# Softmax-free attention with an FP4 gate: one store and eight loads for the reciprocals of a group, in place of four and sixteen

## The reference

```
xn = layernorm(src)
# attention branch, 16 heads of 64
Q = elu(xn @ Wq + bq) + 1 ;  K = elu(xn @ Wk + bk) + 1 ;  V = xn @ Wv + bv
KV = einsum('bshd,bshm->bhdm', K, V)
Z  = 1 / (einsum('bshd,bhd->bsh', Q, K.sum(axis=1)) + 1e-6)
o  = einsum('bshd,bhdm,bsh->bshm', Q, KV, Z)
x  = layer_norm(xn + o @ Wo + bo)
s  = layer_norm(x + gelu(x @ W1 + b1) @ W2 + b2)
# gate branch: rows and weights rounded to FP4 in blocks of 16
g  = silu( fp4_linear( silu(fp4_linear(xn, w_gate)) * fp4_linear(xn, w_up), w_down ) )
out = src + s * g
```

## Time and profile before

| | us |
|---|---|
| median of 3 runs | 1647.81 (1647.04 to 1648.1) |
| the profiled execution | 1644.95 |
| its span, first to last instruction | 1643.2 |
| TensorE busy | 1604.9 (98%) |
| VectorE busy | 1280.4 (78%) |
| ScalarE busy | 980.1 (60%) |
| GpSimd busy | 783.3 (48%) |

### The profile page before, as it was taken

The page is one execution under the profiler, slowest core; times in us unless marked ns, Lnnn a source line. Parts: engine busy times, 40 slices in busy tenths (PEclk is TensorE's granted clock), DMA queues, the critical chain, the costliest instruction groups (busy, mean ns, idle before and its releaser), DMA issues.

```text
span 1643.2 us, 30638 instructions
## 1 busy us (share of the span) xinstructions
PE 1604.9 (98%) x10977; PEld 1440.9 (88%) x10977; DVE 1280.4 (78%) x2485; ACT 980.1 (60%) x1770; POOL 783.3 (48%) x750
## 2 busy tenths in 40 slices
PE   7999999999899999999999999999999999999997
PEld 6878888888789998999999999989899989999897
DVE  6785664554788797888888887879788888878797
ACT  6665666655564747565665647474656656574743
POOL 4564543434242635444444536364455444363636
PEclk9999999999999999999999999999999999999999
DMA  7422323331501111133121112111121321111110
GB/s 227 136 84 86 104 78 106 103 109 57 186 15 53 52 53 52 53 111 91 47 68 53 52 53 107 53 52 53 52 60 61 104 87 58 53 52 53 52 53 26
DMA packets 92515, 123.46 MB, mean 75 GB/s; under 512 B 13503, under 2 KB 60747, under 8 KB 91342
## 3 DMA queue, kind: packets, MB, share of 16 engines
q1 hardware_dynamic: 92366, 121.51, 23.1%
HBM read 86.86 MB, written 34.62 MB: 74 GB/s over the span
## 4 chain that ended last, share of the span: by engine, by line
PE 68%; DVE 13%; DMA 7%; issue 5%; SPq 3%; ACT 3%; POOL 2%; DVEq 0%; POOLq 0%; ACTq 0%
PE QH L81 11%; PE QH L82 11%; PE QH L83 10%; PE AC L81 5%; PE AC L82 4%; PE AC L83 4%; DMA zb<-z_scratch 4%; PE GU L81 4%; PE GU L83 4%; PE GU L82 4%; DVE QH L1828 2%; PE TT L831 2%; DVE rl L1837 2%; SPq L408 2%; DMA z_scratch<-dn_s 1%
## 5 line engine op out<-in xcount | busy, mean ns | idle before, releaser
L2309 POOL TENSOR_TENSOR hb<-hb,rs_h 128x704 f32<-128x704 f32 x64 | 89.0, 1391 | 206.3 <-DVE rs_h L1680 206.3
L1248 ACT ACTIVATE hb<-GU 128x352 f32<-128x352 f32 x128 | 59.2, 463 | 214.3 <-PE GU L83 214.3
L1201 ACT ACTIVATE rh<-QH 128x512 fp32r<-128x512 f32 x256 | 151.2, 598 | 58.2 <-DVE QH L1828 53.2
L81 PE MATMUL GU<-wgh,xqh 128*128 128x352 f32 x512 | 169.8, 332 | 3.1 <-DVE hb L1673 3.1
L2315 POOL TENSOR_TENSOR hb<-hb,sn_h 128x64 f32<-128x64 f32 x64 | 18.8, 293 | 319.5 <-DVE hb L1685 319.5
L83 PE MATMUL GU<-wgh,xql 128*128 128x352 f32 x512 | 165.0, 322 | 0.0
L82 PE MATMUL GU<-wgl,xqh 128*128 128x352 f32 x512 | 164.9, 322 | 0.0
L1843 DVE TENSOR_TENSOR rl<-QH,rh 128x512 fp32r<-128x512 f32 x128 | 86.0, 682 | 85.8 <-ACT rh L1201 83.7
L81 PE MATMUL AC<-Mh,rh 128*128 128x256 f32 x512 | 145.9, 285 | 1.4 <-ACT rh L1201 0.6
L81 PE MATMUL AC<-w2h,rh 128*128 128x256 f32 x512 | 145.7, 285 | 0.0
L82 PE MATMUL AC<-Ml,rh 128*128 128x256 f32 x512 | 142.4, 278 | 0.0
(11 more groups left out here) (234 smaller groups left out, 5586.0 us busy)
## 6 DMA issues: line engine op xcount, KB each, us to landing
zb<-z_scratch SPq DMA_DIRECT2D x256, 128.0 KB, 3.0
xa<-in_L_attn_src SPq DMA_DIRECT2D x16, 512.0 KB, 4.2
xt_scratch<-xth SPq DMA_DIRECT2D x32, 256.0 KB, 2.7
xt_scratch<-xtl SPq DMA_DIRECT2D x32, 256.0 KB, 3.0
xb<-in_L_attn_src SPq DMA_DIRECT2D x16, 512.0 KB, 4.2
xnTh<-xt_scratch SPq DMA_DIRECT2D x32, 256.0 KB, 4.8
xnTl<-xt_scratch SPq DMA_DIRECT2D x32, 256.0 KB, 5.6
out<-x SPq DMA_DIRECT2D x15, 512.0 KB, 6.6
```

Source lines behind the costliest of these rows:

```text
L81: e.matmul(outp, lh, rh, start=start, stop=False, skip_group_check=check)
L1201: e.activation(RH[j % 4][:], src, ACT.Copy).then_inc(S[sem], 1)
L1248: e.activation(HB[i % 3][:, hf * HALF:(hf + 1) * HALF], gu_bank(i, hf)[:, 0:HALF], ACT.Tanh, scale=0.5).then_inc(S["th"], 1)
L2309: e.tensor_tensor(hb, hb, spread(rs_h[i % 2][:], 44), ALU.mult).then_inc(S["hin"], 1)
```

## The change

The four stores of a group become one over all 128 partitions of `dn_s`, with the partitions that hold no head; `z_scratch` has 32 rows for a group instead of 16, and row 16 to 31 are never read. The two loads of a block become one, whose source is two rows, each repeated 64 times. The waits count 16 for a DMA accordingly. Nothing is moved on the other engines.

```diff
-    z_dram = nc.dram_tensor("z_scratch", [NG, 16, 512], F32, kind="Internal").ap()
+    z_dram = nc.dram_tensor("z_scratch", [NG, 32, 512], F32, kind="Internal").ap()
             def z_out(g):
                 w.wait_ge(S["zi"], 2 * g + 2)
-                for t in range(4):
-                    e.dma_start(z_dram[g, :, t * 128:(t + 1) * 128], dn_s[32 * t:32 * t + 16, :]).then_inc(S["zo"], 16)
+                e.dma_start(z_dram[g].rearrange("h (t c) -> t h c", t=4), dn_s[:]).then_inc(S["zo"], 16)
             def z_in(g, j):
-                w.wait_ge(S["zo"], 64 * (g + 1))
+                w.wait_ge(S["zo"], 16 * (g + 1))
                 w.wait_ge(S["zq"], 8 * g + j - 3)
-                for s in range(2):
-                    e.dma_start(ZB[j % 4][64 * s:64 * s + 64, :],
-                                z_dram[g, 2 * j + s].unsqueeze(0).broadcast_to([64, 512])).then_inc(S[f"zb{j % 4}"], 16)
+                e.dma_start(ZB[j % 4][:], z_dram[g, 2 * j:2 * j + 2].unsqueeze(1).broadcast_to([2, 64, 512])).then_inc(S[f"zb{j % 4}"], 16)
             def den_inverse(g):
                 w.wait_ge(S["dn"], g + 1)
-                w.wait_ge(S["zo"], 64 * g)
+                w.wait_ge(S["zo"], 16 * g)
             def z_mul(g, j):
-                w.wait_ge(S[f"zb{j % 4}"], 32 * (2 * g + j // 4 + 1))
+                w.wait_ge(S[f"zb{j % 4}"], 16 * (2 * g + j // 4 + 1))
```

## The result

The changed kernel took 2168.72 us, median of four executions (2165.18 to 2169.65), beside 1647.95 us for the kernel before (1647.04 to 1648.32): a ratio of 1.3157, 95% interval 1.3134 to 1.318. The profiled execution took 2169.65 us, 1.75 us of it beside the span.

A forecast was written before the change was run, and what follows sets the result against it. TensorE, 98% busy, was taken as the bound, its chain passing through each group's reciprocals. Span 1643.2 + 515 (loads on two engines) + 24 (clock) = 2182 us, 2187 us as run time; range 2110 to 2330.

The forecast's parts named there:

- The bound: In every group the chain leaves TensorE through the reciprocals; a stall of TensorE pushes the kernel's end back by nearly as much.
- Two engines and four: New load (2 against 128) runs on two engines, new store (4 against 128) on four; with small clock price, chance 0.78.
- the rival in which only the store is cut and a load keeps 16 engines: Store over four engines, loads over 16: some 0.3 us won a group, 1643 us; chance 0.04.
- 85 ns a row: One engine's time for a 2 KB row of the zb loads, ends 82 and 107; last product 32.2 us later, 515 us.
- The store, gain 0: One store into z_scratch lands when the fourth did before: gain 0, ends 0.4 us gained or lost.
- What lies beside: TensorE has no work to do ahead during the slow loads, so 32.2 us a group go on the path.
- The clock: TensorE's clock probably falls to 1.2 GHz between products; its return costs 1.5 us a group (0 to 3.9), 24 us.
- the rival of sixteen engines: Loads run on sixteen engines after all, 0.7 us a block; 9 us gained, 1639 us (1634 to 1643); chance 0.10.
- The rival in which the clock stays low through most of the 56 us: Low clock behind each group's last product costs 10 us and more a group: 2320 us; chance 0.06.

The follow-up runs named there:

- every kernel of the table: Thirteen kernels, the change and twelve follow-ups, each set beside the kernel before by shift of the last product and of the rest; measured differences from -19.1 to 590.3 us.
- with four engines: Changed kernel's loads, each head's row stored twice by four stores so the load's source leads with 4: 1835.46 us, ratio 1.1137 to the kernel before.
- The experiments with 4, 8 and 16: Changed kernel's eight loads, row copies stored by four stores so the source leads with 4, 8 or 16: 1835.46, 1689.28 and 1666.80 us.
- the kernel with 60 zero matmuls: Changed kernel with zero matmuls filling TensorE's waits in groups 1 to 14, 22 in two places and 60 in the last: 2140.85 us, ratio 1.2981.
- The kernel with one head for all partitions: Changed kernel, each load's source one row repeated 128 times, leaving out each pair's second head: 1629.96 us, ratio 0.9884 to the kernel before.
- with eight copies: Changed kernel's loads, each head's row stored 8 times by four stores so the load's source leads with 16: 1666.80 us, ratio 1.0097.

## Why the prediction came out

It was right in its mechanism, and its terms come out of the trace nearly as written; 2187 us was forecast and 2168.72 measured, 18 us less. That the number came so near is in part luck: the loads were put some 26 us too high and the clock 8 us too low, and the two errors offset each other.

- **The bound.** That the products' chain carries a group was right: each microsecond by which the last one moved was a microsecond of the group, 16 times, in every kernel of the table.
- **Two engines and four.** Right, by 16 completions for eight loads and 4 for the store. The same counts refute the rival in which only the store is cut and a load keeps 16 engines. The experiments with 4, 8 and 16 show that it is the leading dimension, and not the repeat, the bytes or the number of issues.
- **85 ns a row.** 83 ns measured (5.31 us over 64 rows), 84 ns with four engines. This is the first term that was mis-sized: the last product started 47.26 us behind the reciprocal, 48.6 forecast; +30.6 us a group instead of +32.2, 489 us instead of 515. The rest of the gap is the store's 0.3 us below and the start before, 16.67 us as a mean where I took group 4's 16.4. The value at full pace from the earlier trace rows, 82 ns, fitted; the 107 ns of the earlier trace rows, from packets of small shares that share engines with others, would have been wrong for a train.
- **The store, gain 0.** It landed at 2.46 us, 0.3 us earlier. A 512-byte packet took 29 ns on its four engines, not the at most 41 from which I worked. Alone it made the kernel 0.4% faster; the interval, 0.9947 to 0.9974, leaves out no change, if narrowly.
- **What lies beside.** Right: between the products TensorE had the two at_steps of each pair and the turns beside them, and nothing else. The last two gaps of group 4 were 6.14 us (ahead of the fifth and sixth step) and 4.93 us (ahead of gate_up).
- **The clock.** Right in kind: it fell in each group and came back behind the last product, at 7.6 us. Its price was 2.0 us a group, about 32 us in all (15 x 2.0, and 2.3 behind the last group's), and not 1.5 and 24; the kernel with 60 zero matmuls got back 28, in the 14 groups that have them.
- **The rival that was too small.** The kernel with one head for all partitions is the rival of sixteen engines. I had priced it at 9 us gained, from TensorE's waits of 8.7 us; it gained 19. TensorE's idle time, span less busy, fell by what I took, from 1643.2 - 1604.9 = 38.3 to 1626.5 - 1597.7 = 28.8 us. But its busy time fell as well, by 7.2 us, for the same 10977 matmuls. The starts of matmuls in the two traces show where. Counted from the start of the matmul ahead, those of `at_step` that read Mh and `rh` start 5.7 us earlier in all, and of this only 1.3 us had been booked as idle; those of `turn_h` start 10.3 us earlier, where 7.8 us had been idle. Together that is 16.0 of the 16.7 us by which the span is shorter. In a train they start 0.12 us apart and each lasts 0.28 us, by ends that are modelled, so a start that is late by less than the difference shows no idle time. The table of waits undercounts what a late product costs by such pieces; the shift of the last product, 1.13 us x 16 = 18 us, holds them.

The rival in which the clock stays low through most of the 56 us is refuted by 923.80 to 977.70 at full clock.

## What to carry to other kernels

Before two DMAs are made one, compare the leading sizes of both sides as the built program has them. A source that leads with 2 put a transfer of 256 KB on two engines and cost 520 us, where loads of the same bytes that lead with 128 on both sides, in the kernel that leaves out the second head, went with 19 us gained over the kernel before. Count the completions in a stretch of the trace, and price a stall by the shift of the work that ends the chain and not by the idle time that the table of waits shows.

## What the runs showed of the hardware beyond this

- An engine's time for a row in a train: 83 to 84 ns for 2 KB, 45 ns for 1 KB, 29 ns for 512 bytes as stored over four engines. Copies made in a store aren't free: with eight copies, a 512-byte packet took 56 ns on average instead of 32, and the last of four stores landed 4.3 us behind the reciprocal instead of 2.8.
- A SyncE issue took 0.32 us for a load of one repeated row over 128 partitions, 0.45 to 0.60 us for one of 64 partitions, and about 0.5 us with two rows of source. Once the loads on two engines had piled up, the issue itself lasted 5 us, from the fourth in the group on (group 4); with four engines the longest of that group lasted 0.96 us. A long issue can be the sign of slow transfers and not their cause.
- The clock fell to 0.50 behind 4.8 us without a matmul though 2.7 us of them at full clock stood before that gap, and it stayed full over a gap of 0.41 us that followed 7.2 us of work.
